# Every fourth unit's turned attention weights leave PSUM through ScalarE, as 255 less the weight, with a constant product to make up for it

## What is computed

```python
def _fq(x, delta, zp, n_bits):
    xi = _round_ste(x / delta) + zp
    xq = jnp.clip(xi, 0.0, 2.0 ** n_bits - 1.0)
    return (xq - zp) * delta
...
sim = jnp.einsum('bhid,bhjd->bhij', _fq(q, dq, 128.0, 8), _fq(k, dk, 128.0, 8)) * SCALE
attn = jax.nn.softmax(sim, axis=-1)
out = jnp.einsum('bhij,bhjd->bhid', _fq(attn, dw, 0.0, 8), _fq(v, dv, 128.0, 8))
```

## Time and profile before

| | |
|---|---|
| Time before, median of 3 runs | 3313.78 us (3312.22 to 3323.18) |
| The profiled execution, its own time | 3312.55 us |
| Its span, first to last instruction | 3310.7 us |
| PE busy | 2915.5 us (88%) |
| DVE busy | 2120.6 us (64%) |
| POOL busy | 1769.6 us (53%) |
| ACT busy | 1499.0 us (45%) |
| Mean granted TensorE clock | 0.935 of full speed |

### The profile page before, as it was taken

One profiled execution on the slowest core, in us unless ns is written; L12 is line 12 of the kernel. 1 busy time (PEld: TensorE's weight loads), 2 busy tenths in 40 slices (PEclk: granted clock), 3 DMA queues, 4 the chain that ended last, 5 costly groups with the idle time before them and its releaser, 6 DMA issues.

```text
span 3310.7 us, 50798 instructions
## 1 busy us (share of the span) xinstructions
PE 2915.5 (88%) x19712; PEld 2124.5 (64%) x19712; DVE 2120.6 (64%) x3543; ACT 1499.0 (45%) x2178; POOL 1769.6 (53%) x1695
## 2 busy tenths in 40 slices
PE   7676686897889999899989899899988999899998
PEld 6555444565667656667767656666777756666777
DVE  4457595784565587687565587687565588688521
ACT  5332363663433365374334265375334266276321
POOL 3555484785555186385355186386364277377321
PEclk9888756998999999999999989999999999999999
DMA  8654103235543313324352412334353322232444
GB/s 275 235 196 148 57 2 115 102 135 191 166 169 107 132 52 134 134 97 152 122 193 89 157 67 103 118 119 153 131 195 102 142 81 100 86 141 93 163 164 154
DMA packets 199758, 436.40 MB, mean 132 GB/s; under 512 B 94944, under 2 KB 103392, under 8 KB 182368
## 3 DMA queue, kind: packets, MB, share of 16 engines
q1 hardware_dynamic: 199520, 433.15, 36.7%
HBM read 363.38 MB, written 65.54 MB: 130 GB/s over the span
## 4 chain that ended last, share of the span: by engine, by line
PE 56%; POOL 17%; DVE 11%; issue 6%; ACT 6%; DMA 2%; SPq 1%; POOLq 0%; DVEq 0%; ACTq 0%
PE psum L1719 17%; PE psum L1721 15%; PE psum L1720 15%; POOL w1b L997 6%; PE psum L2015 4%; POOL rec L992 2%; PE psum L2003 2%; DVE e L1606 2%; PE psum L2029 1%; ACT psum L1188 1%; POOL u_lo L1016 1%; POOL x L912 1%; POOL w_lo L900 1%; POOL fw_lo L1004 1%; DMA fw_lo<-pieces 1%
## 5 line engine op out<-in xcount | busy, mean ns | idle before, releaser
L1295 ACT ACTIVATE e<-e,nb 128x1024 f32<-128x1024 f32 x512 | 588.4, 1149 | 340.7 <-DVE e L1606 338.5
L1606 DVE TENSOR_SCALAR_CACHE_REDUCE e<-psum,nscale 128x1024 f32<-128x1024 f32 x512 | 653.3, 1279 | 86.2 <-POOL w1b L997 49.0
L997 POOL TENSOR_SCALAR w1b<-e,rec 128x1024 f16<-128x1024 f32 x512 | 572.9, 1119 | 96.4 <-POOL rec L992 58.3
L1719 PE MATMUL psum<-h_hi,fw_hi 128*128 128x512 f32 x1024 | 459.3, 448 | 30.7 <-DVE h_lo L1380 10.0
L1619 DVE TENSOR_SCALAR w1T<-psum 128x1024 bf16<-128x1024 f16 x512 | 352.8, 689 | 95.0 <-PE psum L2015 91.9
L1721 PE MATMUL psum<-h_hi,fw_lo 128*128 128x512 f32 x1024 | 411.3, 402 | 0.0
L1720 PE MATMUL psum<-h_lo,fw_hi 128*128 128x512 f32 x1024 | 411.2, 402 | 0.0
L2015 PE MATMUL psum<-ident,w1b 128*128 128x128 f16 x4096 | 343.7, 232 | 72.7 <-POOL w1b L997 38.9
L2015 PEld LDWEIGHTS psum<-ident,w1b 128*128 128x128 f16 x4096 | 253.2, 103 | 238.5 <-issue 140.8
L906 POOL TENSOR_TENSOR rstd<-ve,mhalf 128x1 f32<-128x1 f32 x128 | 86.6, 677 | 477.8 <-DVE ve L1486 477.8
L1478 DVE TENSOR_TENSOR x<-psum,x 128x512 f32<-128x512 f32 x224 | 152.3, 685 | 231.7 <-PE psum L1721 230.8
(11 more groups left out here) (181 smaller groups left out, 6041.6 us busy)
## 6 DMA issues: line engine op xcount, KB each, us to landing
fw_hi<-pieces SPq DMA_DIRECT2D x168, 512.0 KB, 3.3
fw_lo<-pieces SPq DMA_DIRECT2D x168, 512.0 KB, 4.3
w_hi<-kept SPq DMA_DIRECT2D x45, 1024.0 KB, 5.0
w_lo<-kept SPq DMA_DIRECT2D x45, 1024.0 KB, 7.7
mixed<-mixed SPq DMA_DIRECT2D x32, 1024.0 KB, 5.3
fbias<-in_fside_Bx16xSxS SPq DMA_DIRECT2D x64, 256.0 KB, 3.2
unsplit<-in_L_xattn_ff_w SPq DMA_DIRECT2D x24, 512.0 KB, 5.2
pieces<-fw_hi SPq DMA_DIRECT2D x24, 512.0 KB, 2.7
```

Source lines behind the costliest of these rows:

```text
L997: pool.tensor_scalar(w1b[u % NH][:], e1[u % NE][:], rec1[:, u % 8:u % 8 + 1], HALF, ALU.mult, ALU.add).then_inc(w1_ready.sem, 1)
L1295: act.activation(e1[s % NE][:], e1[s % NE][:], ACT.Exp, bias=nb1[:, s % NE:s % NE + 1], scale=-1.0, accum_out=sum1[:, s % 8:s % 8 + 1]).th ...
L1606: emptied_bank(dve.tensor_scalar(e1[s % NE][:], psum[:, i:i + 2, :].rearrange("p i n -> p (i n)"), nscale[:, 0:1], LARGEST, ALU.mult, ALU.min,
L1719: pe.matmul(o, s_hi, m_hi, start=first, stop=False)
```

## The change

In slots whose unit has `u % 4 == 3` (the fourth head of each group of four), DVE no longer takes the turned weights out of bank 4. ACT does, behind the exponential of the same slot and ahead of what it hosts. It computes Relu(1279 - x), which is 255 less the weight, with 0 for a weight above 255. The weighted sum of that head then gets, for each key tile, a second product of the same values with a block of -255 (one column, broadcast to 128), so that the sum is the negative of what it was, and the scale of these 32 rows is negated once at the start. The rest, and the other three of four units, stay as they are.

```diff
+TURNED_ROUND = 3
...
+        def wait_weights_used(eng, n, g):
+
+            if g % 4 == 3:
+                wait_filled(eng, ("a1", n, g // 4))
+            else:
+                eng.wait_ge(w1T_used.sem, w1T_used.at((n, g)))
...
                         act.activation(e1[s % NE][:], e1[s % NE][:], ACT.Exp, bias=nb1[:, s % NE:s % NE + 1], scale=-1.0,
                                        accum_out=sum1[:, s % 8:s % 8 + 1]).then_inc(exp1_done.sem, 1)
+                    u = s - LAG_T
+                    if 0 <= u < UNITS and u % 4 == TURNED_ROUND:
+                        key = ("p1T", n, u)
+                        wait_filled(act, key)
+                        if u >= 8:
+                            wait_weights_used(act, n, u // 4 - 2)
+                        act.activation(w1T[u % 8][:].rearrange("p k q -> p (k q)"), bank(bank_of(key)).bitcast(FP16), ACT.Relu,
+                                       bias=above[:, 0:1], scale=-1.0).then_inc(emptied[bank_of(key)], 1)
...
+            dve.memset(above[:], HALF + W_HIGH)
+            dve.memset(all_high[:], -W_HIGH)
...
-                dve.tensor_tensor(unit_v[:, i:i + 1], dw, dv, ALU.mult)
+                link(dve.tensor_tensor(unit_v[:, i:i + 1], dw, dv, ALU.mult))
             landed()
+            rest = slice(DH * TURNED_ROUND, DH * TURNED_ROUND + DH)
+            dve.tensor_scalar(unit_v[rest, 0:1], unit_v[rest, 0:1], -1.0, None, ALU.mult)
...
-                    if 0 <= u < UNITS:
+                    if 0 <= u < UNITS and u % 4 != TURNED_ROUND:
...
-                                ins = pe.matmul(bank(5)[DH * h:DH * h + DH, t * P:t * P + P], v1[:, k, hd:hd + DH],
-                                                w1T[4 * (g % 2) + h][:, k, :], start=(k == 0), stop=(k == KEYT - 1))
+                                o = bank(5)[DH * h:DH * h + DH, t * P:t * P + P]
+                                last = k == KEYT - 1
+                                ins = pe.matmul(o, v1[:, k, hd:hd + DH], w1T[4 * (g % 2) + h][:, k, :], start=(k == 0),
+                                                stop=last and h != TURNED_ROUND)
+                                if h == TURNED_ROUND:
+                                    ins = pe.matmul(o, v1[:, k, hd:hd + DH], all_high[:, 0:1].broadcast_to((P, P)), start=False,
+                                                    stop=last)
```

More of the change, by code:

```diff
@@ L303, in build @@
         rounder = sb("rounder", [P, 1])
+        above = sb("above", [P, 1])
+        all_high = sb("all_high", [P, 2], BF16)
         ident = sb("ident", [P, P])
@@ L1613, in self_attention @@
                         if u % 4 == 0 and u >= 8:
[L1614 to L1618, removed]
+                            wait_weights_used(dve, n, u // 4 - 2)
                         emptied_bank(dve.tensor_scalar(w1T[u % 8][:].rearrange("p k q -> p (k q)"),
```

## The result

The changed kernel took 3540.9 us (median of 4 runs, 3526.31 to 3548.54) against 3318.48 beside it: a ratio of 1.0668, 95% interval 1.0643 to 1.0692. That is slower by some 222 us; the forecast was slower by 196. Of all executions behind this document one is left out of its ratio, as slow by its granted clock: the fourth of the six of the last experiment, 4231.22 us at a mean clock of 0.642, where the other five had 0.938 to 0.941; no run tells why.

The account below looks back on a forecast made before the run. PE was taken to bound chunk 3, with no engine having much room in chunk 2; bank 4 decides. Stage terms 61 + 84 + 36 + 15 = 196 on 3312.55 gave about 3508 us, range 3430 to 3585.

Parts of the forecast that it names:

- Bank 4 opens 1.69 us later: Bank 4, after DVE begins the scores of slot a: opens at 3.73 us instead of 2.04, behind ACT's exponential and eviction.
- transposes of b: PE's transposes in the slot after slot a: cannot start before 4.44 us after PE began slot a.
- slot a: In each round of four slots, the slot whose eviction moves to ACT (s % 4 = 0).
- The products: PE's weighted sum: added products cost 0.23 us a part, 0.46 a round; at 1.2 GHz 0.45 a part.
- Chunk 0: Self-attention stage of chunk 0, mostly at 1.2 GHz: rounds of 10.61 against 8.34 us, 36 us more.
- Chunk 1: Self-attention stage of chunk 1, paced by POOL's splits at 10.32 us a round: 15 us more.
- Chunks 3, 5, 7: PE-bound stages: rounds of 10.45 against 9.09, 22 us, plus 6 for two Gelus delaying ACT; 28 each, together 84.
- Chunks 2, 4, 6: Self-attention stages: rounds of 9.84 against 8.57 us, 20 us each, three times 61 in all.
- Rival 1: All stages: the lateness is covered and only the products cost, 51 us in all, 3363 us; chance 0.11.
- rival 2: Chunks 0, 2, 4 and 6: DVE is the bound and is relieved, 38 us faster, 3274 us; chance 0.03.
- Rival 3: ACT: Relu not in Exp's table, so two table loads a round, 328 us more in the loop, 3836; chance 0.02.
- Rival 4: Chunks 2, 4 and 6: the clock falls where PE now stands, 80 us more, 3588 us; chance 0.05.

Follow-up runs that it names:

- the last experiment: Changed kernel with PE doing the score products five times in slot b of chunks 2, 4 and 6: 3512.38 us, ratio 1.0601.
- the second and third experiment: Changed kernel without the added products: 3503.63 us, ratio 1.0576; changed kernel with ACT's eviction ahead of the exponential in slot a: 3410.31 us, ratio 1.0298.
- the sixth: Changed kernel with ACT's eviction ahead of the exponential, no added products, units u % 4 == 1 instead of 3, cap at 255 left out: 3343.04 us, ratio 1.0099.

## Why the prediction was right, and where its sizes were off

The range (3430 to 3585) held, and the mechanism was the forecast one. One sign of being right was missed: rounds were to be 9.5 to 10.6 us in every stage, and their means were 10.1 in chunk 0, 10.8 in chunk 2, 11.1 in chunk 1 and 11.2 in chunk 3. For chunk 1 the sum itself had more than the sign allowed (10.32 + 15 / 16 = 11.26); what is missing in chunks 2 and 3 is below.

- *Bank 4 opens 1.69 us later.* Right: the transposes of b began 4.42 us into slot a (4.44), undisturbed rounds of chunk 2 took 9.4 (9.49), and exchanging two instructions on ACT gave 123 to 131 us back. The 0.04 us between the end of the transposes and DVE's eviction, a term of the 4.44, stands in none of the rows before the prediction; in the changed kernel's slot above the transposes end at 1216.29 + 0.44 = 1216.73 and DVE starts at 1216.77.
- *The eviction's price*, 1.11 us between bounds of 1.05 and 1.36: 1.097 on average. The Trainium skill's formula for it ("ScalarE: Activation LUTs", What ACT_TABLE_LOAD costs) gave an estimated 1.13; the measured figure is the lower one, and it decides.
- *The products*, 0.23 us a part: right at full clock (0.34 to 0.57). In chunk 0 too high, 0.42 a round for 0.9, with the clock up from 0.54 to 0.64. In all 39 us alone, 30 to 37 taken out of the changed kernel.
- *Chunk 0*: 24.5 / 14 x 16 = 28 us, forecast 36. Its clock rose from 0.54 to 0.67, and the forecast had priced all of PE's work there at 1.2 GHz.
- *Chunk 1*: 11.5 / 14 x 16 = 13 us, forecast 15.
- *Chunks 3, 5, 7*: 29.7 / 14 x 16 = 34 us in chunk 3 and as much in 5 and 7, forecast 28. The term of the Gelus was mis-sized: 3 us each were the stop alone (3.42 measured), and with the half clock behind it a round took 15.8 where others took 10.1 to 10.8. Leaving the pass out took 10 us from chunk 3.
- *Chunks 2, 4, 6*: 31.0 / 14 x 16 = 35 us in chunk 2, forecast 20; 34 and 30 in chunks 4 and 6. This is the largest miss. The term lacked the clock: with the stops filled the same stage has (140.39 - 119.94) / 14 x 16 = 23 us. I had the clock as a rival of 80 us at a chance of 0.05; it came, but as an addition of 8 to 11 us in the 14 rounds of each of these stages.
- *The total*: added up so, the eight stages make 243 us where the profiled executions are 236 apart and the ratio says 222; the forecast was 196. That 196 came as near owes something to terms that were off both ways: chunk 0 was too high by 8 and chunk 1 by 2, the other six stages were too low by 6 to 15 each.
- *What DVE gives up gains nothing.* Right: even with the eviction early, at the better place and without the products, chunk 0 was at 117.23 against 116.83.
- *Rivals.* Rival 1 (lateness covered) fell by the result and by the second and third experiment, rival 2 (faster) by the result and by the sixth. Rival 3: the Relus took 1.09 to 1.12 us, the group of L1313 has no table load beside it, and the run has 58 loads, as before. Rival 4 is above.

What stays open: the 30 us that the better-placed version still costs (44 in its profiled execution) are only in part located. The 14 rounds of the eight stages hold 24 of the 44, among them a Gelu round that is 3 us longer in each of chunks 2, 4 and 6 and 4 us in chunk 1; the other 20 lie outside these rounds, in pieces of up to 4 us between the stages, and no run tells them apart. Why the clock fell at some stops of about the same length and not at others is open too.

## What to carry to other kernels

Before work is moved to the engine with the lowest busy share, look at what that engine does in the same slot and in which order: an operation that frees a shared bank must not stand behind one that itself waits. Price the move by the moment at which the resource opens, from the start of the slot, against the moment at which the next user comes; here 4.4 against 2.8 us, once in four slots, outweighed 88 us of relieved DVE. And an engine that is nearly always busy may gain the kernel nothing when it is relieved (DVE in chunk 0 was busy 106.34 of 116.83 us, and 98.18 of 117.23 afterwards): take its work away first with as little put in its place as can be, and see whether anything moves.

## What the hardware showed that I had not expected

- Stops on PE cost clock on top of time. In chunk 2, with stops of up to 2.1 us, the mean granted clock was 0.96 before, 0.88 with the stops, and 0.98 with the stops filled by repeated products, which made the whole kernel faster by 22 to 28 us while PE did more. In chunk 3 a round with a stop of 3.42 us had 0.78, the stretch before it 1.00.
- In chunk 0, where the clock is mostly 1.2 GHz, 128 further products of 128 columns raised its mean from 0.54 to 0.64, and taking them out of the changed kernel lowered it from 0.67 to 0.53. The added products cost 0.42 us a round, where the same columns at 1.2 GHz take 0.9, and leaving them out gave 0.45.
- Two products on the same 32-column group follow each other at the pitch of 128 columns while the other three groups run beside: eight steps where there were four, 0.57 us for 0.34, also when one operand is a single column broadcast.
